# Layer 1 of a cross network: from tiles of products that stand still in the array to banks of h1·W1 that are multiplied by x and added afterwards

## The reference

```
e = stack(tbl_f[ids[:, f]] for 64 fields)            # x: 512 x 64 x 16, f32
h = x
for W in (W0, W1, W2):                               # W0: 64*64 x 128; W1, W2: 64*128 x 128
    h = einsum('bid,bjd,ijn->bnd', x, h, W.reshape(64, -1, 128))
    outs.append(h)
z = sum(concatenate(outs, axis=1), axis=-1)          # 512 x 384
h = relu(concatenate([z, dense_ctx], 1) @ W_top1 + b_top1)
h = relu(h @ W_top2 + b_top2)
y = h @ W_top3                                       # 512 x 1
```

## Time and profile before

| | |
|---|---|
| time, median of 3 runs (lowest, highest) | 1259.45 us (1255.41, 1260.35) |
| the profiled execution: its span, first to last instruction | 1255.5 us |
| busy: TensorE, VectorE, GpSimd, ScalarE | 94%, 76%, 71%, 49% |
| granted TensorE clock, mean | 0.988 |
| HBM read and written | 112.74 MB, 6.29 MB |

### The profile page before, as it was taken

One profiled execution on the slowest core, in us unless ns is written; L12 is line 12 of the kernel. 1 busy time (PEld: TensorE's weight loads), 2 busy tenths in 40 slices (PEclk: granted clock), 3 DMA queues, 4 the chain that ended last, 5 costly groups with the idle time before them and its releaser, 6 DMA issues.

```text
span 1255.5 us, 15492 instructions
## 1 busy us (share of the span) xinstructions
PE 1184.6 (94%) x4404; PEld 751.1 (60%) x4404; DVE 957.6 (76%) x843; ACT 614.4 (49%) x788; POOL 890.8 (71%) x596
## 2 busy tenths in 40 slices
PE   1589999999999999989999999999999999899999
PEld 0255656656566665646567665656657675565656
DVE  0588888879795797978887588888878678697940
ACT  0253645546372464726454273645556164464732
POOL 5467878787876678777787667878787667873740
PEclk9889999999999999999999999999999999899999
DMA  5641514132234422314153441414233451322320
GB/s 154 191 147 22 155 33 130 58 90 95 53 131 115 130 91 69 111 35 138 30 152 93 109 135 28 155 34 125 63 90 115 105 168 36 105 79 61 121 76 1
DMA packets 99824, 120.16 MB, mean 96 GB/s; under 512 B 42097, under 2 KB 46961, under 8 KB 99346
## 3 DMA queue, kind: packets, MB, share of 16 engines
q1 hardware_dynamic: 87602, 109.61, 28.2%
q0 software_dynamic: 8192, 2.11, 2.2%
q10 hardware_dynamic: 3936, 7.34, 1.8%
HBM read 112.74 MB, written 6.29 MB: 95 GB/s over the span
## 4 chain that ended last, share of the span: by engine, by line
POOL 46%; PE 25%; issue 23%; DMA 3%; ACT 1%; DVE 0%; POOLq 0%; ACTq 0%; SPq 0%
POOL lo_sb L514 29%; POOL rows_sb L473 15%; PE acc L785 5%; PE acc L799 4%; PE acc L793 4%; PE acc L795 4%; PE acc L771 3%; PE side L823 2%; DMA rhs_ring_sb<-x_scratch 2%; POOL xdiag_sb L484 2%; PE side L816 1%; PE rhs L884 1%; DMA rhs_ring_sb<-h_scratch 1%; PE acc L922 1%; ACT hi_sb L671 0%
## 5 line engine op out<-in xcount | busy, mean ns | idle before, releaser
L514 POOL TENSOR_TENSOR lo_sb<-prod_sb,hi_sb 128x1024 fp32r<-128x1024 f32 x256 | 608.4, 2392 | 200.8 <-ACT hi_sb L671 199.1
L585 DVE TENSOR_TENSOR prod_sb<-x_tiles_sb,rhs 128x1024 f32<-128x1024 f32 x534 | 635.9, 1214 | 125.3 <-PE acc L771 60.8
L793 PE MATMUL acc<-hi_sb,w_hi_sb 128*128 128x512 f32 x768 | 336.2, 438 | 6.8 <-ACT hi_sb L671 6.0
L671 ACT ACTIVATE hi_sb<-prod_sb 128x1024 fp32r<-128x1024 f32 x256 | 270.4, 1056 | 124.6 <-DVE prod_sb L585 64.7
L771 PE MATMUL acc<-prod_sb,w_sb 128*128 128x512 f32 x640 | 284.4, 599 | 34.3 <-DVE prod_sb L560 34.3
L473 POOL DMA_INDIRECT rows_sb<-tables,rows_now_sb x256 | 242.7, 948 | 92.3 <-issue 79.2
L795 PE MATMUL acc<-hi_sb,w_lo_sb 128*128 128x512 f32 x768 | 304.7, 397 | 0.0
L623 ACT ACTIVATE rhs<-rhs_ring_sb 128x512 f32<-128x512 f32 x192 | 118.4, 618 | 325.0 <-DVE prod_sb L585 196.0
L799 PE MATMUL acc<-lo_sb,w_hi_sb 128*128 128x512 f32 x768 | 245.7, 401 | 21.5 <-POOL lo_sb L514 21.4
L785 PE MATMUL acc<-prod_sb,w_raw_sb 128*128 128x512 f32 x512 | 240.4, 592 | 0.0
L771 PEld LDWEIGHTS acc<-prod_sb,w_sb 128*128 128x128 f32 x640 | 121.1, 192 | 181.3 <-issue 164.9
(11 more groups left out here) (40 smaller groups left out, 232.9 us busy)
## 6 DMA issues: line engine op xcount, KB each, us to landing
rhs_ring_sb<-h_scratch SPq DMA_DIRECT2D x128, 256.0 KB
x_tiles_sb<-x_scratch SPq DMA_DIRECT2D x120, 256.0 KB
rhs_ring_sb<-x_scratch SPq DMA_DIRECT2D x60, 256.0 KB
w_sb<-w_rows SPq DMA_DIRECT2D x50, 256.0 KB, 2.8
rows_sb<-tables,rows_now_sb POOLq DMA_INDIRECT x256, 3.5
h_scratch<-h_sb ACTq DMA_DIRECT2D x16, 256.0 KB, 2.3
...
```

Source lines behind the costliest of these rows:

```text
L514: pool.tensor_tensor(lo[:, slot], prod[:, slot], hi[:, e % HI].bitcast(F32), ALU.subtract).then_inc(lo_pool_ready, 1)
L585: dve.tensor_tensor(prod[:, prod_slot(q, g)], *operands(par, a, j % 2), ALU.mult).then_inc(prod_ready, 1)
L671: act.activation(hi[:, e % HI], src, ACT.Copy).then_inc(hi_ready, 1)
L793: pe.matmul(bank, w1_hi[:, w, :], hi[:, e % HI, i, :], start=first and i == 0, stop=False, skip_group_check=True)
```

## The change

Layer 1 is turned round. Within a chunk, take 128 columns (a *block of columns* s of four) and 4 fields i (k of 16): a *place* p = 16 s + k, 64 in a chunk. TensorE computes T = h1ᵀ · W1 for the place: h1 (128 rows j by 128 columns) is the stationary operand, W1 of the four fields (128 x 512) is streamed, and the result, a PSUM bank of 128 columns by 4 x 128 outputs, has the *columns on the partitions*. Both operands are split, so a place is three fp32r products (`fill_bank`). Then h2 for these columns is the sum over all 64 fields of x_i times the i-th quarter of the banks, where x_i is one number per partition. Of the 16 places of a block, ten (`D_IN`) are taken by VectorE (`take_bank`: four instructions of 128 x 128 that multiply and add into `parts`) and six (`A_IN`) by ScalarE (`scale_bank`: four scaled copies into `y`), whose results GpSimd adds in pairs (`add_pairs`). `finish_block` sums the six partial results of a block on VectorE into `h2t`, which is already turned as `form_g` wants it. Four PSUM banks `tps` go round as a ring.

Layer 0 uses all of x against x turned by k fields (`roll`, loaded from a doubled copy of x in DRAM), 8 groups of two tiles, now split, and half a tile in float32 (`w0_end`). All its subtractions are VectorE's. z of layer 1 comes from four small products (`sum_h2`). GpSimd no longer subtracts. The loads of `rhs` (12 a chunk) and `x_tiles` (8) go, and 18 loads of `roll` a chunk come.

The core of the diff (the removed functions are printed above):

```diff
+A_IN = (1, 3, 6, 8, 11, 13)
+D_IN = tuple(k for k in range(KS) if k not in A_IN)
+N_A, N_D = SUB * len(A_IN), SUB * len(D_IN)
...
+L0_AT = (8, 14, 20, 26, 32, 38, 44, 50, 54)
+PROD_AT = tuple(p - 8 for p in L0_AT)
+HI_AT = tuple(p - 6 for p in L0_AT[:SPLIT])
+LO_AT = tuple(p - 4 for p in L0_AT[:SPLIT])
+H1_HI_AT, H1_LO_AT = 57, 58
+G_AT = (4, 16)
+Z2_AT = 22
...
+FINISH_AT = 8
...
+                for i in range(2):
+                    first = x_of(t)[4 * g + 2 * i:4 * g + 2 * i + 1, :]
+                    src = bass.AP(first.tensor, first.offset, [[CH, 2], [CH, FIELDS], [1, CH]])
+                    sp.dma_start(roll[:, slot, i, :], src).then_inc(roll_loaded[slot], 16)
...
+                if at == 3:
+                    pool.wait_ge(a_done, t * N_A + 2 * (pair + 1))
+                    if q >= 0 or s > 0:
+                        pool.wait_ge(y_step, before)
+                    pool.tensor_tensor(ysum[:], y[:, (pair - 1) % Y_RING], y[:, pair % Y_RING], ALU.add).then_inc(y_step, 1)
+                if at == 5:
+                    pool.wait_ge(a_done, t * N_A + 2 * (pair + 1))
+                    pool.wait_ge(y_step, before + 1)
+                    pool.tensor_tensor(ysum[:], ysum[:], y[:, pair % Y_RING], ALU.add).then_inc(y_step, 1)
+                    pool.wait_ge(y_step, before + 2)
+                    pool.tensor_tensor(ysum[:, 0:CH], ysum[:, 0:CH], ysum[:, CH:2 * CH], ALU.add).then_inc(y_step, 1)
+                    pool.wait_ge(y_step, before + 3)
+                    if q >= 0 or s >= 2:
+                        pool.wait_ge(h2t_ready, t * SUB + (s - 1))
+                    pool.tensor_tensor(parts[:, s % 2, QUAD:PARTS, :].rearrange("p u n -> p (u n)"), ysum[:, 0:2 * NF],
+                                       ysum[:, 2 * NF:4 * NF], ALU.add).then_inc(y_step, 1)
...
+                if g == SPLIT:
+                    dve.tensor_tensor(prod[0:FIELDS, slot, 0, :], roll[0:FIELDS, ring, 0, :], xx_ps[0:FIELDS, 0, :],
+                                      ALU.mult).then_inc(prod_ready, 1)
+                    return
+                dve.tensor_tensor(prod[:, slot], roll[:, ring], xx_ps[:].to_broadcast([P, 2, CH]), ALU.mult).then_inc(prod_ready, 1)
+
+            def subtract(q, t, g):
+                slot = ring_place(q, g, 2)
+                dve.wait_ge(hi_ready, t * SPLIT + (g + 1))
+                dve.tensor_tensor(lo[:, slot], prod[:, slot], hi[:, g % 2].bitcast(F32), ALU.subtract).then_inc(lo_ready, 1)
...
+                dve.wait_ge(t_ready, t * PLACES + (p + 1))
+                for u in range(QUAD):
+                    i = QUAD * k + u
+                    bank = tps[:, p % RING, u * NF:(u + 1) * NF]
+                    part = parts[:, s % 2, u, :]
+                    scale = xcol[:, (q + 1) % 2, s, i:i + 1]
+                    if k == D_IN[0]:
+                        done = dve.tensor_scalar(part, bank, scale, None, ALU.mult)
+                    else:
+                        if u % 2 == 0:
+                            dve.wait_ge(d_half, t * (2 * N_D) + (2 * d - 1 + u // 2))
+                        done = dve.scalar_tensor_tensor(part, bank, scale, part, ALU.mult, ALU.add)
+                    if u % 2 == 1:
+                        done.then_inc(d_half, 1)
+
+            def finish_block(q, t, s):
+                dve.wait_ge(d_half, t * (2 * N_D) + 2 * len(D_IN) * (s + 1))
+                dve.wait_ge(y_step, t * (SUB * STEPS_OF_SUM) + (s + 1) * STEPS_OF_SUM)
+                if s == 0 and q >= 0:
+                    dve.wait_ge(z2_filled, t)
+                dve.tensor_reduce(h2t[:, (q + 1) % 2, s, :], parts[:, s % 2].rearrange("p u n -> p n u"),
+                                  AX_X, ALU.add).then_inc(h2t_ready, 1)
...
+                for u in range(QUAD):
+                    i = QUAD * k + u
+                    done = act.activation(y[:, pair % Y_RING, half * CH + u * NF:half * CH + (u + 1) * NF],
+                                          tps[:, p % RING, u * NF:(u + 1) * NF], ACT.Copy,
+                                          scale=xcol[:, (q + 1) % 2, s, i:i + 1])
+                done.then_inc(a_done, 1)
...
+                    pe.matmul(acc[:], w0_end[:], prod[0:FIELDS, ring_place(q, g, 2), 0, :], start=False, stop=True,
+                              skip_group_check=True).then_inc(prod_used, 1)
+                    return
+                slot = ring_place(q, g, 2)
+                pe.wait_ge(hi_ready, t * SPLIT + (g + 1))
+                for i in range(2):
+                    pe.matmul(acc[:], w0_hi[:, 2 * g + i, :], hi[:, g % 2, i, :], start=g == 0 and i == 0, stop=False,
+                              skip_group_check=True)
+                    pe.matmul(acc[:], w0_lo[:, 2 * g + i, :], hi[:, g % 2, i, :], start=False, stop=False,
+                              skip_group_check=True)
+                pe.wait_ge(lo_ready, t * SPLIT + (g + 1))
+                for i in range(2):
+                    mm = pe.matmul(acc[:], w0_hi[:, 2 * g + i, :], lo[:, slot, i, :], start=False, stop=False,
...
+                if q >= 0 or p >= RING:
+                    old = (p - RING) % PLACES
+                    back = 0 if p >= RING else -1
+                    if is_a(old):
+                        pe.wait_ge(a_done, t * N_A + (back * N_A + a_before(old) + 1))
+                    else:
+                        pe.wait_ge(d_half, t * (2 * N_D) + 2 * (back * N_D + d_before(old) + 1))
+                cols, of = slice(s * P, (s + 1) * P), slice(k * CH, (k + 1) * CH)
+                bank = tps[:, p % RING, :]
+                pe.matmul(bank, h1_hi[:, par, cols], w1_hi[:, of], start=True, stop=False, skip_group_check=True)
+                pe.matmul(bank, h1_hi[:, par, cols], w1_lo[:, of], start=False, stop=False, skip_group_check=True)
+                pe.matmul(bank, h1_lo[:, par, cols], w1_hi[:, of], start=False, stop=True,
+                          skip_group_check=True).then_inc(t_ready, 1)
```

More of the change, by code:

```diff
@@ L59 @@
 W1_PARTS = 8
 W2_I, W2_SLOTS = 4, 2
[L61 to L66, removed]
-HIDDEN1, HIDDEN2, DENSE = 512, 256, 16
[L71 to L90, removed]
+F_LOADS = FIELDS // W2_I
+L0_AT = (8, 14, 20, 26, 32, 38, 44, 50, 54)
+PROD_AT = tuple(p - 8 for p in L0_AT)
@@ L101, in kind_of @@
[L101 to L117, removed]
-    (c, a, i) for c in range(N_H) for a in range(0, N_X, PAIR) if KINDS[c][a // PAIR] != "raw" for i in range(PAIR))}
@@ L146, in groups_before @@
-def groups_before(t, g):
-    return t * N_G + (len(L0) + g)
-def rhs_before(t, j):
-    return t * N_R + (N_Y + j)
-def prod_slot(q, g):
-    return (len(L0) + N_G * (q + 1) + g) % PROD
-assert PER_BLOCK * N_G % PROD == 0 and N_SPLIT % HI == 0
-def back(groups, start, g, depth, *kinds):
-    here = places(groups, *kinds)
-    ahead = L0 if start else GROUPS
-    there = [x - len(ahead) for x in places(ahead, *kinds)]
-    every = there + here
-    at = every.index(g) - depth
-    return every[at] if at >= 0 else None
@@ L175, in side_before, with is_a, a_before, d_before @@
-def side_before(bt, q):
-    if q < 0:
-        return 0
-    return bt * (4 * PER_BLOCK + 1) + (1 + 4 * q)
+def is_a(p):
+    return p % KS in A_IN
+def a_before(p):
+    return sum(1 for x in range(p) if is_a(x))
+def d_before(p):
+    return sum(1 for x in range(p) if not is_a(x))
 def build(nc, ins, out):
@@ L517, in _ @@
+            def chunk(bt, q, t):
+                for p in range(PLACES):
+                    if p in GATHER_AT and gathers(t):
+                        if p == GATHER_AT[0]:
+                            pool.wait_ge(x_stored, t * 32 + 32)
+                        gather(t + 2, (q + 1) % 2, GATHER_AT.index(p), gathered[(q + 1) % 2])
+                    if is_a(p):
+                        add_pairs(q, t, p)
+                    if p == XDIAG_AT:
+                        diagonal(q, t)
             pool.wait_ge(ids_loaded, 32)
@@ L612, in _ @@
             each_chunk(dve, chunk)
-            dve.wait_ge(h2_copied, CHUNKS)
-            sum_over_d(1, h2, CHUNKS - 1)
+            finish_block(PER_BLOCK - 2, CHUNKS - 1, SUB - 1)
         @block.scalar
         def _(act):
-            def copy_rhs(slot, bank, loads, free):
-                act.wait_ge(rhs_loaded[slot], loads)
-                if free is not None:
-                    act.wait_ge(prod_ready, free)
-                act.activation(rhs[:, bank, :], rhs_ring[:, slot, :], ACT.Copy).then_inc(rhs_ready, 1)
```

895 lines of the change are left out of this document (403 added, 492 removed).

## The result

The changed kernel takes 1741.3 us (median of 4 runs, 1739.5 to 1742.6) against 1259.9 before: ratio 1.384, 95% interval 1.381 to 1.388. Forecast was 1184, faster than before; the slowest case with a price was 1306.

What follows compares the result with a forecast made beforehand. TensorE was taken to bound the kernel, with VectorE nearly equal: 65.5 start + 12 plain chunks of 65.5 + 3 of 77.5 + 49.5 last chunk + 46.5 end = 1180 us, 1184 as median; range 1150 to 1215.

Steps and rivals of the forecast that it cites:

- the slowest case with a price: VectorE's small instructions pay 90 ns for a per-partition scalar operand: 1306 us; chance 0.25, shared with the sequencer case.
- The loads fall from 20 to 18 of 256 KB a chunk and stay hidden: Loads from DRAM: two fewer a chunk, hidden behind the engines' work, no time added.
- VectorE's term of 59.1 us a chunk: VectorE's work in a chunk, of which 33.6 us are the 160 small instructions.
- the finish: VectorE's `finish_block`, reading 768 elements with a stride: 0.87 to 1.8 us, taken as 1.4, four a chunk.
- VectorE's spacing, 0.21 us: Time between starts of VectorE's 128-element instructions in `take_bank`; bounds 0.20 to 0.30 us, 160 a chunk.
- the rival: Per-partition scalar costs VectorE 90 ns, as on ScalarE: spacing 0.29 to 0.30, 1306 us; chance 0.25 with the sequencer case.
- Disturbance: VectorE's subtractions and GpSimd's additions, both reading SBUF, wait for each other: 3.5 us a chunk, 1229 us; chance 0.14.
- TensorE's sum and the ring: TensorE's work 59.9 us a plain chunk; waits around the four PSUM banks and chunk turn bring it to 65.5.
- break-even is a plain chunk of 70.5 us: The plain chunk at which the changed kernel would equal the old one, a spacing of about 0.26 us.
- ScalarE and GpSimd: Their work in a chunk: 39 us and 49 us, neither bounding the kernel.
- The wait of the finish for GpSimd: `finish_block` waits for GpSimd's last sum, which was expected some 9 us before being needed; priced at nothing.
- The start: Time before layer 1 of the first chunk: h1 split at about 60 us, layer 1 taken to start at 65.5.

Runs made afterwards that it cites:

- e5_tiny_sums: e1_sixteen with GpSimd's additions of 1024 and 512 columns cut to 8 columns, output not the reference's; 1245.0 us.
- e4_constant_scale: e1_sixteen with the constant 1.5 in place of the column of x in VectorE's 160 small instructions a chunk, output not the reference's; 1200.3 us.
- e8_both: e1_sixteen with both the constant 1.5 as VectorE's scale and GpSimd's additions cut to 8 columns, output not the reference's; 1172.0 us.
- e10_first_place: e1_sixteen with VectorE's first place of each block done in one instruction of 512 columns in place of four; everything computed; 1266.3 us.
- e1_sixteen: The changed kernel with each turned tile of x loaded as two transfers of 64 rows in place of one of 2 x 64 x 512; 1295.0 us.
- e6_eight: e1_sixteen with eight of a block's sixteen places on ScalarE in place of six, and GpSimd adding four pairs in place of three; 1299.9 us.

## Why the prediction was wrong

- **The step that failed** is "The loads fall from 20 to 18 of 256 KB a chunk and stay hidden". It counted transfers and bytes and not the shape of their source. Loads at 50 GB/s need 84 us a chunk, over any engine's sum, and the plain chunk became 92.1 us. It cost 443 of the 1737 us (446 by the medians), and none of the rivals or bounds held it: the queue of SyncE was never walked through. Without it the forecast still fails, in its direction too: 1295, slower than before, because VectorE's term of 59.1 us a chunk is 71.6. Of these 12.5, 7.5 are the spacing (160 · 0.047), 3.8 the stretched subtractions (8 · 0.47) and 0.5 the finish (1.52 us, taken as 1.4).
- **VectorE's spacing, 0.21 us**: for an instruction with a constant it is right (0.200). With the pointer it is 0.257: the rival took ScalarE's 90 ns, the price on VectorE is 57. Alone it makes 1245 (e5_tiny_sums, plain chunk 68.7), not 1306, and doesn't reach slower.
- **Disturbance**, a rival with a plain chunk of 69 us and 1229 in all, 49 over the sum. The stretch itself was priced right: 0.44 us a subtraction (40% of 1.1), measured 0.47 (1.68 less 1.21). What it costs the kernel was not: alone, in e4_constant_scale, it makes 1200 with a plain chunk of 64.3, 28 over e8_both, since VectorE has room there. It costs 50 (1295.0 against 1245.0, 4.3 a plain chunk) only beside the pointer. What the list of rivals lacked is that both can come together: 123 us over e8_both, where 73 and 28 alone make 101.
- **TensorE's sum and the ring.** With both lifted, a plain chunk is 63.5 us (forecast 65.5) and a W2 chunk 77.4 (77.5), the whole 1172 (1184). TensorE's work was 61.9, not 59.9 (0.6 of it is `sum_h2`, taken as 0.4 and measured at 1.0), and the losses beside it 1.6, not 5.6. That the whole came so near is in part luck: the fifteen chunks are 21 us shorter than forecast, the start, the last chunk and the end together 11 us longer (172.5 of the 1169.7, forecast 161.5). VectorE's sum was 59.1 and is 58.0. For the same reason "break-even is a plain chunk of 70.5 us" was a little too high: e10_first_place, whose plain chunks are 70.5 on average, takes 0.9% more than the kernel before.
- **ScalarE and GpSimd** at 39 and 49: 39.7 and 49.5 in the chunk of e1_sixteen. The wait of the finish for GpSimd, priced at nothing, is 2.6 us in 1295 there; it grows only with eight places (38.2 in e6_eight).
- **The start.** The first rounding of h1 was taken at about 60; in e1_sixteen it is at 69.1. What takes the 9 us was not looked into.
